# Output experts of the gated attention, batches 0 to 2: from all experts on all rows to rows sorted by chosen expert

## The chip, the cores and the metric

The program runs on one core of one Trainium2 chip. The metric is the device time of one execution in microseconds (us). Below, PE is TensorE, DVE is VectorE, ACT is ScalarE, POOL is GpSimd and SP is SyncE, which issues most of the DMAs.

## The reference, cut to what matters

```python
def _L0_ffn_ref(x, w_q, w_k, w_gate, value_experts, output_experts):
    ...
    gates = jax.nn.sigmoid((x @ w_gate).reshape(b, n, HEADS, EXPERTS).transpose(0, 2, 1, 3))
    sel = jnp.argmax(gates, axis=-1)
    gm = jax.nn.one_hot(sel, EXPERTS, dtype=x.dtype) * gates
    values = jnp.einsum('bhne,ehdk,bnd->bhnk', gm, value_experts, x)
    ...
    out = jnp.einsum('bhij,bhjk->bhik', attn, values)
    out = jnp.einsum('bhne,ehkd,bhnk->bhnd', gm, output_experts, out)
    return out.sum(axis=1)
```

This is the second of four layers: a cross-attention ("a"), this gated causal self-attention ("b"), a second cross-attention of 16 heads ("c"), and a layer of 32 routed experts ("d"). There are 4 batches of 512 tokens of 256 numbers. Layer b has 8 heads of 64 numbers, and for each token and head one of 8 experts is chosen: `gm` has one number per (token, head, expert) that is not zero. The last einsum turns a head's 64 numbers into 256 by the chosen expert's 64x256 matrix, scales them by its gate, and the sum over heads is added to x.

## The kernel before, in words

Layers a and b are in `attentions_ab`, which runs batch by batch: `attention_a(b)`, `head_b(b)`, `attention_b(b)`. Each engine has its own hand-written list of steps, and the lists meet at semaphores. Layers c and d follow in functions of their own.

In `attention_b` the four pairs of heads are worked one after the other. A pair's stretch of PE's list holds: 8 value units of the next pair (`unit`, L856: tokens of one tile times the 8 experts' value weights, 512 columns; DVE multiplies by the gates, L1209, and adds the 8 experts up, L1213); the transposes of the probabilities (`turn_b`, L794), read out by ACT (L1103) and DVE (L1319); the next pair's scores (`scores_b`, L773 and L778), whose maxima DVE takes (L1200) and whose exponentials ACT makes (L1095); probabilities times values (`values`, L827), read out by ACT into `boT` (L1125), which holds both heads of the pair, 64 partitions each; and the output experts. For these, DVE splits the gates over the softmax's sums into three bf16 parts (`split_gates`), PE transposes them (`gates`, L803) and spreads expert e's gates over the partitions (`select`, L814), DVE multiplies `boT` by them (`gate_out`, L1332), and PE multiplies each product by the expert's weights (`out`, L840):

```python
for t in range(NT):
    mm = pe.matmul(ps[:, 6 + t // 2, (t % 2) * D:(t % 2 + 1) * D], og[:, e, t * P:(t + 1) * P],
                   oxB[:, p, e, :], start=first and t % 2 == 0, ...)
```

All pairs and experts of a batch add up in PSUM banks 6 and 7, and DVE adds the sum to x at the start of the next batch (`add_out`, L1416). An fp32 matmul of the code stands as two MATMUL records in the trace; a transpose stands as one. The units of pairs 1 to 3 have a single PSUM bank (2), so a unit waits until DVE has multiplied the one before.

`unit` 0 to 7 and `pair` 0, 1, 2 come first; `last_pair` (pair 3) has no units and is filled with the scores of the next batch's layer a. In batch 3 `ending_pair` and the `quarter`s and `half`s of layer c take that place. SP loads the contexts (`load_context`, L516 to L520), x (L511) and the weights, and stores x (L581). POOL has the norms and little else in these batches.

## Time and profile before

| | |
|---|---|
| median of 3 runs | 2100.2 us (2096.24 to 2101.73) |
| profiled execution: span, from first to last instruction | 2122.9 us |
| the profiled execution's own time | no figure beside its span; the span stands for it |
| PE busy | 1982.3 us, 93% |
| DVE busy | 1269.1 us, 60% |
| ACT busy | 893.8 us, 42% |
| POOL busy | 528.3 us, 25% |
| DMA | 184.97 MB, 87 GB/s over the span |

Busy times of an engine are a union over the span. Layers a and b of the four batches lie between about 130 and 1100 us. A busy PE isn't PE at its peak: the granted clock tells the level.

### The profile page before, as it was taken

The page shows a single profiled execution, that of the slowest core. Times are in us where ns is not written, and L with a number is a line of the kernel's source. Part 1 is how long each engine was busy: PE and PEld are TensorE (multiplying, and loading weights), DVE is VectorE, ACT ScalarE, POOL GpSimd, SP SyncE. Part 2 cuts the span into 40 slices and gives each one's busy share as a digit, 9 for nine tenths or more (in the row PEclk, how much of TensorE's full clock was granted, in tenths as well). Part 3 has the DMA queues.
Part 4 walks back from the last instruction along what each step waited for, and adds up shares of the span by engine and source line. Part 5 has one row for each costly group of instructions (what it writes and reads, how often), then busy time and mean ns, then how long its engine had stood idle before and what let it go on. Part 6 is the DMA issues. An engine that isn't in the chain of part 4 may idle for free. (4 is left out here: it accounts for less than half of the span.)

```text
span 2122.9 us, 27241 instructions
## 1 busy us (share of the span) xinstructions
PE 1982.3 (93%) x10186; PEld 1100.5 (52%) x10186; DVE 1269.1 (60%) x2541; ACT 893.8 (42%) x1791; POOL 528.3 (25%) x454
## 2 busy tenths in 40 slices
PE   7989999999999999899989999999999999965994
PEld 5666567745676567746643333433433343334773
DVE  5423765366633764367777777777776777741343
ACT  3412211221112211121118888778777977841221
POOL 4311000210001000000034223236324531426664
PEclk9999999999999999999999999999999999986997
DMA  8743000110001000110226383345335432215986
GB/s 286 213 200 111 1 1 11 45 43 1 1 21 62 1 1 11 34 28 16 44 79 129 85 259 81 80 120 123 90 70 146 104 57 43 73 62 164 251 182 157
DMA packets 101531, 184.97 MB, mean 87 GB/s; under 512 B 38151, under 2 KB 62549, under 8 KB 100120
## 3 DMA queue, kind: packets, MB, share of 16 engines
q1 hardware_dynamic: 83000, 153.24, 26.8%
q0 software_dynamic: 18400, 30.00, 6.3%
q8 instruction: 81, 1.33, 0.3%
q14 instruction: 50, 0.41, 0.1%
HBM read 127.38 MB, written 65.25 MB: 91 GB/s over the span
## 5 line engine op out<-in xcount | busy, mean ns | idle before, releaser
L2216 DVE CUSTOM_DVE_ANT_0 ps<-ps,maskN 128x801 f32<-128x801 f32 x480 | 467.7, 1014 | 129.5 <-PE ps L2009 126.3
L2189 ACT ACTIVATE d_prob<-ps 128x512 f32<-128x512 f32 (+1 forms) x832 | 473.4, 597 | 158.3 <-PE ps L2039 153.2
L856 PE MATMUL ps<-vx_or_keys,b_xT 128*128 128x512 f32 x512 | 240.3, 597 | 4.9 <-DVE val_or_prob L1209 4.9
L840 PE MATMUL ps<-oxB,og_or_pT 128*128 128x256 f32 x1024 | 241.1, 380 | 0.0
L2051 PE MATMUL ps<-d_prob,vaug 128*32 128x512 f32 (+1 forms) x1664 | 226.6, 610 | 0.3 <-ACT d_prob L2189 0.3
L840 PEld LDWEIGHTS ps<-oxB,og_or_pT 128*128 128x128 f32 x1024 | 190.5, 190 | 37.4 <-issue 11.2
L2038 PE MATMUL ps<-maskT,identb 128*128 128x512 bf16 (+1 forms) x498 | 192.2, 386 | 5.7 <-DVE d_oN L2248 1.7
L1095 ACT ACTIVATE prob_or_gate<-ps,b_mx 128x512 f32<-128x512 f32 (+3 forms) x128 | 66.1, 525 | 289.4 <-DVE b_mx L1200 289.4
L2185 ACT CAST ps<-maskT 128x512 f32<-128x512 bf16 (+1 forms) x310 | 185.6, 599 | 0.0
L260 POOL DMA_INDIRECT table<-xr,slot x128 | 128.6, 1005 | 177.5 <-PE ps L2039 140.8
L1209 DVE TENSOR_TENSOR val_or_prob<-ps,b_gm 128x512 f32<-128x512 f32 x128 | 88.4, 691 | 107.1 <-PE ps L856 107.0
L856 PEld LDWEIGHTS ps<-vx_or_keys,b_xT 128*128 128x128 f32 x512 | 93.5, 190 | 85.5 <-issue 77.5
L1213 DVE TENSOR_REDUCE val_or_prob<-val_or_prob 128x64 f32<-128x512 f32 x128 | 132.3, 1034 | 4.4
L2039 PE MATMUL ps<-raw,kS 99*128 99x512 bf16 (+1 forms) x312 | 115.7, 387 | 1.7 <-ACT ps L2185 1.7
L2038 PEld LDWEIGHTS ps<-maskT,identb 128*128 128x128 bf16 (+1 forms) x498 | 49.7, 100 | 123.0 <-issue 36.6
L1913 POOL TENSOR_SCALAR maskT<-c_rawT 128x512 bf16<-128x512 int32 (+1 forms) x52 | 100.2, 1926 | 49.0 <-PE ps L2039 42.2
L2039 PE MATMUL ps<-vx_or_keys 99*128 99x512 bf16 (+1 forms) x260 | 99.2, 385 | 1.9 <-ACT ps L2185 1.9
L2039 PE MATMUL ps<-qS,vx_or_keys 99*128 99x512 bf16 (+1 forms) x260 | 98.9, 384 | 1.9 <-ACT ps L2185 1.9
L670 PE MATMUL ps<-og_or_pT,raw 128*128 128x128 f32 (+1 forms) x832 | 97.6, 275 | 0.0
L640 PE MATMUL ps<-maskN,kS 128*128 128x512 f32 (+1 forms) x256 | 95.0, 519 | 1.7 <-PEq L98 1.7
L670 PEld LDWEIGHTS ps<-og_or_pT,raw 128*128 128x128 f32 (+1 forms) x832 | 95.4, 192 | 1.5 <-issue 1.5
L1332 DVE TENSOR_TENSOR og_or_pT<-b_oT,ps 128x512 f32<-128x512 f32 x128 | 81.9, 681 | 18.2 <-PE ps L814 18.2
(321 smaller groups left out, 2807.8 us busy)
## 6 DMA issues: line engine op xcount, KB each, us to landing
c_rawT<-in_maskT SPq DMA_DIRECT2D x24, 512.0 KB
vx_or_keys<-k_parts SPq DMA_DIRECT2D x60, 200.1 KB, 7.2
k_parts<-x_k SPq DMA_DIRECT2D x16, 600.4 KB
table<-xr POOLq DMA_DIRECT2D x16, 578.0 KB
e_buf<-table SPq DMA_DIRECT2D x32, 289.0 KB
...
```

The costliest lines, as they stand in the source:

```text
L260: g.indirect_dma_start(out=k.table[:, :], out_offset=bass.IndirectOffsetOnAxis(ap=k.slot[:, j:j + 1], axis=0), in_=k.xr[:, t, :], in_offse ...
L670: mm = pe.matmul(ps[:, 6, m * P:(m + 1) * P], k.ctxNA[0:KW[i], i, m * P:(m + 1) * P], pT[0:KW[i], i, :], start=i == 0 and m == 0, stop=i = ...
L840: mm = pe.matmul(ps[:, 6 + t // 2, (t % 2) * D:(t % 2 + 1) * D], og[:, e, t * P:(t + 1) * P], oxB[:, p, e, :], start=first and t % 2 == 0, ...
L856: mm = pe.matmul(ps[:, bank, :], xTB[:, c, t * P:(t + 1) * P], vxB[:, c, h, :], start=c == 0, stop=c == NC - 1)
L1213: v.tensor_reduce(val[:, t, h // 2 % 2, h % 2, :], tmp[:, u % 2, :].rearrange("p (e d) -> p d e", e=EB), AX_X, ALU.add).then_inc(val_sum, 1)
L1913: g.tensor_scalar(maskT[0:KW[i], i, :], rawT[0:KW[i], u % 2, i % 2, :], 0.0, MASKED, ALU.is_equal, ALU.mult).then_inc(biasT, 1)
L2038: pe.matmul(ps[0:w, BANKS[u], :], k.identb[0:w, 0:w], maskT[0:w, i, :], start=True, stop=False)
L2039: pe.matmul(ps[0:w, BANKS[u], :], kS[G % NS][0:KROWS + 3, h, i * P:i * P + w], qS[G % NS][0:KROWS + 3, h, :], start=False, stop=True, skip ...
L2051: mm = pe.matmul(ps[VW * h:VW * (h + 1), ACC, :], vaug[0:w, G % 2, i, h, :], prob[0:w, T % 2, h, :], start=i == 0, stop=i == NKT - 1)
L2185: nc.scalar.copy(ps[0:w, BANKS[later], :], maskT[0:w, i, :]).then_inc(mask_a, 1)
L2189: nc.scalar.activation(prob[0:w, T % 2, h, :], ps[0:w, BANKS[GH * T + h], :], ACT.Exp, scale=SCALE_C).then_inc(exped, 1)
L2216: v.tensor_tensor_reduce(banks, banks, maskN[:, t, MO[half]:MO[half] + w], 1.0, -3.0e38, ALU.add, ALU.max, mp[:, t, h, half:half + 1]).the ...
```

## The change

`SORTED` is 3: for batches 0 to 2 the output experts work on sorted rows; batch 3 keeps the code above. For each head the 512 tokens are put in blocks of 128 rows with one expert's weights; 8 experts need at most `BLOCKS` = 11 of them (`ROWS` = 1408). Once in a batch PE counts (`counts`, 14 matmuls of 64 columns in bf16) and DVE works out each token's slot, its row numbers and each block's expert (`place`, 23 instructions in five pieces between the units 3 and 7, and one copy of the picks). Then for each pair Q = 4b+p: PE transposes `boT` back to tokens (`turn_rows`, 4), DVE scales by gate over sum (`weigh`) into `rows` (`write_rows`), POOL scatters them to DRAM with 8 indirect DMAs of 128 rows of 256 bytes, SP loads all 11 blocks (`load_sorted`, 704 KB) and, for 11 blocks and 2 heads, reads the expert's number into a register and loads 64x256 weights (`load_experts`). One pair later PE transposes the 11 blocks (`turn_sorted`, 3 groups), ACT reads them out (`read_sorted`), PE multiplies 22 times with 64 rows and 256 columns (`out_sorted`, 6 chunks), ACT reads each chunk out (128x1024) and stores it with two DMAs (`read_blocks`), POOL gathers 8 times 128 rows of 1 KB (`gather`), and DVE adds them to x with 8 additions of 128x256 (`add_back`), two pairs after Q.

`pair` becomes `sorted_pair`; `last_pair` has `turn_sorted` and `out_sorted` of pair 2 in the place of `out`, `select` and `gates`. Pair 3's sorted work stands in `sorted_between`, after the next batch's `attention_a` and ahead of its `head_b`. x has three buffers, in place of two; layer c's first queries move from batch 1 to batch 2; `oxB` is loaded once batches 0 to 2 are done with its memory; both `sorted_in` tensors are filled with zeros at the start.

```diff
+SORTED = NB - 1
+BLOCKS = (S + EB * (P - 1)) // P
+ROWS = BLOCKS * P
+CHUNKS = -(-BLOCKS // 2)
+PLACING = 23
...
+            def load_experts(b, p):
+                Q = PAIRS * b + p
+                sp.wait_ge(placed, PLACING * (b + 1))
+                if Q >= 2:
+                    sp.wait_ge(blocks_mm, CHUNKS * (Q - 1))
+                for j in range(BLOCKS):
+                    for a in range(2):
+                        at = (2 * p + a) * BLOCKS + j
+                        e = sp.value_load(of_block[b % 2][0:1, at:at + 1], min_val=0, max_val=EB - 1)
+                        half = slice(DB * a, DB * (a + 1))
+                        sp.dma_start(we[half, Q % 2, j, :], A["B_ox"][half, p, bass.ds(e, 1), :].rearrange(
+                            "p o n -> p (o n)")).then_inc(ld_we[Q % 2], 16)
+            def load_sorted(b, p):
+                Q = PAIRS * b + p
+                sp.wait_ge(scattered[Q % 2], 16 * 2 * NT * (Q // 2 + 1))
+                if Q:
+                    sp.wait_ge(sorted_mm, 3 * Q)
+                sp.dma_start(inS, k.sorted_in[Q % 2].rearrange("(j p a) d -> p j (a d)", p=P, a=2)).then_inc(ld_sorted, 16)
...
+                if b < SORTED:
+                    for p in range(PAIRS):
+                        load_experts(b, p)
+                        load_sorted(b, p)
+                        if p == 1 and b >= 1:
+                            keep_x(b - 1)
+                else:
+                    sp.wait_ge(blocks_mm, CHUNKS * EARLIER)
+                    for p in range(PAIRS - 1):
+                        sp.dma_start(oxB[:, p], A["B_ox"][:, p]).then_inc(ld_ox, 16)
                     first_group()
...
+            def scatter(b, p):
+                Q = PAIRS * b + p
+                g.wait_ge(placed, PLACING * (b + 1))
+                g.wait_ge(rows_v, Q + 1)
+                if Q >= 2:
+                    g.wait_ge(ld_sorted, 16 * (Q - 1))
+                for t in range(NT):
+                    for a in range(2):
+                        at = t * HB + 2 * p + a
+                        g.indirect_dma_start(out=k.sorted_in[Q % 2][:, :], out_offset=bass.IndirectOffsetOnAxis(
+                            ap=to_sorted[b % 2][:, at:at + 1], axis=0), in_=rows[:, t, a, :], in_offset=None,
...
+            def gather(Q):
+                b, p = divmod(Q, PAIRS)
+                all_kept(g, Q + 1)
+                for t in range(NT):
+                    n = NT * Q + t
+                    if n >= 2:
+                        g.wait_ge(added, 2 * (n - 1))
+                    for a in range(2):
+                        at = t * HB + 2 * p + a
+                        g.indirect_dma_start(out=back[:, t % 2, a, :], out_offset=None, in_=k.sorted_out[Q % 2][:, :],
+                                             in_offset=bass.IndirectOffsetOnAxis(ap=from_sorted[b % 2][:, at:at + 1], axis=0),
...
+                if b >= 1:
+                    g.wait_ge(nb.turned, b + 1)
+                for p in range(PAIRS):
+                    if b >= 1 and p < 2:
+                        gather(PAIRS * b - 2 + p)
+                    if b < SORTED:
+                        if p >= 2:
+                            gather(PAIRS * b - 2 + p)
+                        scatter(b, p)
...
+            def turn_sorted(Q, g):
+                if g == 0:
+                    pe.wait_ge(ld_sorted, 16 * (Q + 1))
...
+                if g == 2:
+                    pe.wait_ge(sorted_a, 3 * Q + 1)
+                for i, j in enumerate(range(4 * g, min(4 * g + 4, BLOCKS))):
+                    mm = pe.transpose(ps[:, 3 + g % 2, i * P:(i + 1) * P], inS[:, j, :], k.ident[:, :])
+                mm.then_inc(sorted_mm, 1)
+            def out_sorted(Q, c):
+                b, p = divmod(Q, PAIRS)
+                bank = 6 if p < PAIRS - 1 or c % 2 == 0 else 0
+                if c == 0:
+                    pe.wait_ge(sorted_a, 3 * (Q + 1))
+                    pe.wait_ge(ld_we[Q % 2], 16 * 2 * BLOCKS * (Q // 2 + 1))
...
+                before = CHUNKS * Q + c - (1 if p < PAIRS - 1 or c == 0 else 2)
+                if before >= 0:
+                    pe.wait_ge(blocks_a, before + 1)
+                for i, j in enumerate(range(2 * c, min(2 * c + 2, BLOCKS))):
+                    for a in range(2):
+                        half = slice(DB * a, DB * (a + 1))
+                        mm = pe.matmul(ps[:, bank + a, i * D:(i + 1) * D], inT[half, j, :], we[half, Q % 2, j, :],
+                                       start=True, stop=True)
+                mm.then_inc(blocks_mm, 1)
...
+            def sorted_between(b):
+                Q = PAIRS * b - 1
+                for g in range(3):
+                    turn_sorted(Q, g)
+                for c in range(CHUNKS):
+                    out_sorted(Q, c)
...
             for b in range(NB):
                 attention_a(b)
+                if b:
+                    sorted_between(b)
                 head_b(b)
...
+            def read_sorted(Q, g):
+                if g == 0 and Q % PAIRS < PAIRS - 1:
+                    act.wait_ge(placed, PLACING * (Q // PAIRS + 1))
+                act.wait_ge(sorted_mm, 3 * Q + g + 1)
+                w = min(4, BLOCKS - 4 * g)
+                nc.scalar.copy(inT[:, 4 * g:4 * g + w, :], ps[:, 3 + g % 2, 0:w * P].rearrange("p (j n) -> p j n", n=P)).then_inc(
+                    sorted_a, 1)
+            def read_blocks(Q, c):
+                p = Q % PAIRS
+                bank, n = 6 if p < PAIRS - 1 or c % 2 == 0 else 0, CHUNKS * Q + c
+                act.wait_ge(blocks_mm, n + 1)
+                if n >= 2:
+                    act.wait_ge(kept[c % 2], 32 * (n // 2))
+                if c < 2 and Q >= 2:
+                    act.wait_ge(gathered[0], 64 * (Q - 1))
+                    act.wait_ge(gathered[1], 64 * (Q - 1))
+                w = min(2, BLOCKS - 2 * c)
+                o = outS[p < PAIRS - 1][c % 2]
+                nc.scalar.copy(o[:, :, 0:w, :], ps[:, bank:bank + 2, 0:w * D].rearrange("p a (j n) -> p a j n", n=D)).then_inc(
+                    blocks_a, 1)
+                act.wait_ge(blocks_a, n + 1)
+                for a in range(2):
+                    half = k.sorted_out[Q % 2][ROWS * a:ROWS * (a + 1), :].rearrange("(j p) n -> p j n", p=P)
+                    nc.scalar.dma_start(half[:, 2 * c:2 * c + w, :], o[:, a, 0:w, :]).then_inc(kept[c % 2], 16)
...
                 for p in range(PAIRS):
                     Q, more = PAIRS * b + p, p + 1 < PAIRS
+                    behind = p >= 1 and b < SORTED
                     read_turned(Q)
+                    if behind:
+                        read_sorted(Q - 1, 0)
                     if more:
                         probabilities(b, p + 1, 0)
                     act.wait_ge(bpv_mm, Q + 1)
-                    if Q:
-                        act.wait_ge(gated, EB * Q)
+                    if 1 <= Q <= EARLIER:
+                        act.wait_ge(rows_mm, Q)
...
                     nc.scalar.copy(boT[:, :], ps[:, 5, :]).then_inc(bo_ev, 1)
+                    if behind:
+                        read_sorted(Q - 1, 1)
+                        read_sorted(Q - 1, 2)
+                        read_blocks(Q - 1, 0)
                     if more:
                         probabilities(b, p + 1, 1)
+                    if behind:
+                        for c in range(1, 4):
+                            read_blocks(Q - 1, c)
+                    if more:
                         probabilities(b, p + 1, 2)
+                    if behind:
+                        for c in range(4, CHUNKS):
+                            read_blocks(Q - 1, c)
             for b in range(NB):
                 attention_a(b)
+                if b:
+                    for g in range(3):
+                        read_sorted(PAIRS * b - 1, g)
+                    for c in range(CHUNKS):
+                        read_blocks(PAIRS * b - 1, c)
                 attention_b(b)
...
+            def write_rows(b, p):
+                Q = PAIRS * b + p
+                v.wait_ge(weighted, Q + 1)
+                v.wait_ge(rows_mm, Q + 1)
+                if Q:
+                    v.wait_ge(scattered[(Q - 1) % 2], 16 * 2 * NT * ((Q - 1) // 2 + 1))
+                v.tensor_tensor(rows, ps[:, 4, :].rearrange("p (t a d) -> p t a d", t=NT, a=2),
+                                weight.unsqueeze(3).to_broadcast([P, NT, 2, DB]), ALU.mult).then_inc(rows_v, 1)
+            def add_back(Q, t):
+                b, n = Q // PAIRS, NT * Q + t
+                x = k.xx[b % 3][:, t, :]
+                v.wait_ge(gathered[t % 2], 32 * (n // 2 + 1))
+                for a in range(2):
+                    if n or a:
+                        v.wait_ge(added, 2 * n + a)
+                    v.tensor_tensor(x, x, back[:, t % 2, a, :], ALU.add).then_inc(added, 1)
...
+            def sorted_pair(b, p):
+                u, Q = 2 * NT * (p + 1), PAIRS * b + p
+                def add(t):
+                    if Q >= 2:
+                        add_back(Q - 2, t)
+                unit(b, u)
+                turned_b(b, p, 1)
+                turned_b(b, p, 3)
+                unit(b, u + 1)
+                turned_b(b, p, 5)
+                weigh(b, p)
+                maxima(b, p + 1, 0)
+                unit(b, u + 2)
+                add(0)
+                unit(b, u + 3)
+                write_rows(b, p)
+                add(1)
+                unit(b, u + 4)
+                maxima(b, p + 1, 1)
+                unit(b, u + 5)
+                add(2)
+                unit(b, u + 6)
+                maxima(b, p + 1, 2)
+                unit(b, u + 7)
+                add(3)
...
```

The order of PE's instructions in batch 0, pair 1, from unit u+4 on. Before (L856 is `unit`, L773 and L778 the scores, L814 `select`, L840 `out`):

```order
L856 MATMUL ps<-vx_or_keys,b_xT 128x512 [waits b_val_mul]
L856 MATMUL ps<-vx_or_keys,b_xT 128x512
L773 MATMUL ps<-b_kT,b_qT 128x384 [waits b_exp]
L773 MATMUL ps<-b_kT,b_qT 128x384
L773 MATMUL ps<-b_kT,b_qT 128x128 x2
L778 MATMUL ps<-causal,identb 128x128 x4
L814 MATMUL ps<-b_gT,sel 128x512 [waits b_gated] x2
L840 MATMUL ps<-oxB,og_or_pT 128x256 [waits b_gated]
L840 MATMUL ps<-oxB,og_or_pT 128x256 x3
L856 MATMUL ps<-vx_or_keys,b_xT 128x512 [waits b_val_mul]
```

Now (L1056 is `unit`, L902 and L907 the scores, L992 `out_sorted`; `e_blocks` counts ACT's readouts):

```order
L1056 MATMUL ps<-vx_or_keys,b_xT 128x512 [waits b_val_mul]
L1056 MATMUL ps<-vx_or_keys,b_xT 128x512
L992 MATMUL ps<-oxB,og_or_pT 128x256 [waits b_val_mul,e_ld_we0,e_sorted]
L992 MATMUL ps<-oxB,og_or_pT 128x256 x3
L902 MATMUL ps<-b_kT,b_qT 128x384 [waits b_exp]
L902 MATMUL ps<-b_kT,b_qT 128x384
L902 MATMUL ps<-b_kT,b_qT 128x128 x2
L907 MATMUL ps<-causal,identb 128x128 x4
L992 MATMUL ps<-oxB,og_or_pT 128x256 [waits e_blocks]
L992 MATMUL ps<-oxB,og_or_pT 128x256 x3
L1056 MATMUL ps<-vx_or_keys,b_xT 128x512 [waits b_val_mul]
```

Where `out` waited for DVE's products, each chunk from the second on waits for ACT's readout of the one before.

ACT's order between the last step of `attention_a(1)` (L435) and layer b's first readout (L1388), where before the change nothing stood in between (`e_kept0` and `e_kept1` count landed stores; the rows L1379 and L1384 come 6 times in all):

```order
L435 COPY a_kb<-ps 128x4 [waits na_kb_mm]
L1365 COPY og_or_pT<-ps 128x512 [waits e_sorted_mm] x2
L1365 COPY og_or_pT<-ps 128x384 [waits e_sorted_mm]
L1379 COPY val_or_prob<-ps 128x1024 [waits rows_gathered0,rows_gathered1,e_kept0,e_blocks_mm]
L1384 DMA sorted_out<-val_or_prob 128x2x256 [waits e_blocks]
L1384 DMA sorted_out<-val_or_prob 128x2x256
...
L1379 COPY val_or_prob<-ps 128x2x256 [waits e_kept1,e_blocks_mm]
L1384 DMA sorted_out<-val_or_prob 128x256 [waits e_blocks]
L1384 DMA sorted_out<-val_or_prob 128x256
L1388 COPY b_xT<-ps 128x512 [waits nb_turned]
```

Six readouts and twelve stores of pair 3 now stand ahead of the copy that the gates, queries and keys of layer b wait for.

SP's order at the start of `load_experts(0, 0)`; the four rows from the register load on come 264 times in the program, 22 times for a pair:

```order
L558 DMA raw<-in_ctx 65x256
L603 TENSOR_LOAD oxB [waits e_placed]
L603 ISA x2
L605 ISA
L605 DMA oxB<-in_B_ox 64x256
L603 TENSOR_LOAD oxB
```

Before, SP had four loads of 1 MB for all batches (L563) in their place.

## Rows read from the trace of the kernel before

**Rows 1.** The page: the span and busy times of the engines.

```profile
span 2122.9 us, 27241 instructions
PE 1982.3 (93%) x10186; PEld 1100.5 (52%) x10186; DVE 1269.1 (60%) x2541; ACT 893.8 (42%) x1791; POOL 528.3 (25%) x454
```

**Rows 2.** Windows: stretch, its length, busy us of PE, PEld, DVE, ACT, POOL; clock; DMA.

```profile
206.90:225.60 18.70, 17.70 (x57) 7.30 (x56) 16.32 (x21) 4.40 (x16) 0.00 (x0) 1.00 0.00 1
225.60:260.30 34.70, 33.35 (x140) 18.40 (x141) 25.59 (x39) 6.42 (x20) 0.00 (x0) 1.00 0.00 0
260.30:298.10 37.80, 37.80 (x169) 23.65 (x168) 25.01 (x38) 6.53 (x20) 0.00 (x0) 1.00 0.00 1
335.90:367.10 31.20, 31.20 (x153) 23.44 (x152) 10.74 (x21) 3.82 (x6) 0.00 (x0) 1.00 0.01 1
```

**Rows 3.** PE's timeline in pair 1 of batch 0: start, length, line, tiles, count.

```profile
260.33 0.93 PE L794 MATMUL ps<-ident,prob_or_gate 128*128 128x128 f32 x7
261.09 1.89 PE L840 MATMUL ps<-oxB,og_or_pT 128*128 128x256 f32 x8
262.82 0.93 PE L794 MATMUL ps<-ident,prob_or_gate 128*128 128x128 f32 x7
...
282.14 0.59 PE L814 MATMUL ps<-b_gT,sel 128*128 128x512 bf16 x2
282.58 1.89 PE L840 MATMUL ps<-oxB,og_or_pT 128*128 128x256 f32 x8
...
289.99 0.70 PE L773 MATMUL ps<-b_kT,b_qT 64*128 64x256 f32 x4
290.62 0.29 PE L778 MATMUL ps<-causal,identb 128*128 128x128 bf16 x2
```

**Rows 4.** Groups on DVE and ACT by form, 200 to 1100 us.

```profile
L1213 DVE TENSOR_REDUCE val_or_prob<-val_or_prob 128x64 f32<-128x512 f32 x128 | 132.3, 1034 | 4.4
L1209 DVE TENSOR_TENSOR val_or_prob<-ps,b_gm 128x512 f32<-128x512 f32 x128 | 88.4, 691 | 107.1 <-PE ps L856 107.0
L1416 DVE TENSOR_TENSOR xx<-xx,ps 128x256 f32<-128x256 f32 x8 | 2.8, 415 | 4.8 <-PE ps L840 4.7
L1229 DVE TENSOR_TENSOR b_gr<-b_gr,gp 128x64 f32<-128x64 f32 x16 | 3.6, 225 | 0.5
L1245 DVE TENSOR_TENSOR prob_or_gate<-prob_or_gate,b_gtop 128x256 f32<-128x256 f32 x3 | 1.3, 425 | 0.1
L1070 ACT ACTIVATE val_or_prob<-ps,a_mx 128x1601 f32<-128x1601 f32 x12 | 19.2, 1597 | 109.0 <-DVE a_mx L1180 109.0
L1125 ACT COPY b_oT<-ps 128x512 f32<-128x512 f32 x16 | 9.4, 586 | 29.3 <-PE ps L827 29.3
```

**Rows 5.** Queries by line: DMA issues (duration ns min/median/max), a register move, landing times.

```profile
L294 SPq DMA_DIRECT2D total<-xr x3: 376/377/386, 1333.9 to 1738.3; - x3
DMA to landing us min/median/max: 2.9/2.9/4.0
L260 POOLq MOVE  x128: 29/29/29, 1410.5 to 1929.7; - x128
L260 POOL DMA_INDIRECT table<-xr,slot x128: 967/975/1607, 1411.3 to 1945.4; - x128
DMA to landing us min/median/max: 2.1/2.1/2.4
L516 SPq DMA_DIRECT2D maskN<-in_ctxT x6: 327/379/433, 160.4 to 641.3; - x6
DMA to landing us min/median/max: 4.2/5.0/7.1
```

**Rows 6.** PE's timeline and windows at the head of batch 3, where PE had waited.

```profile
899.62 0.69 PE L739 MATMUL ps<-ident,og_or_pT 128*128 128x128 f32 x2 [4.61 <-DVE og_or_pT L1159]
901.18 3.65 PE L745 MATMUL ps<-wgB,b_xT 128*128 128x64 f32 x16 [0.87 <-DVE b_xT L1287]
890.00:900.00 10.00, 4.93 (x37) 4.25 (x36) 5.16 (x8) 0.63 (x2) 3.71 (x4) 0.91 0.64 147
900.00:910.00 10.00, 9.13 (x26) 5.83 (x25) 5.17 (x9) 1.57 (x3) 0.00 (x0) 0.58 0.73 97
```

327 lines of the change are left out of this document (271 added, 56 removed).

## The prediction

> **What bounds the kernel now.** I read the page first, for the shares, then the windows by stage, then PE's timeline inside one pair, then the groups of DVE and ACT, and last the DMA issues. The page has PE busy 93% of a span of 2122.9 us [rows 1]. The windows show that in the stretches that the change touches it is full: in a middle pair PE is busy 37.8 of 37.8 us, in the last pair 31.2 of 31.2, while DVE has 25.0 and 10.7 and ACT 6.5 and 3.8 [rows 2]. Only the first units of a batch are another matter: DVE is busy 16.3 of 18.7 us and PE idles there [rows 2]. So in the pairs, work taken from PE is worth its time, as long as what replaces it keeps up; DVE has some 12 us of room in a pair, and ACT, POOL and SP are nearly idle. What has to be read out of the change is what these idle engines are asked to do in series with PE.
>
> **What PE loses and gets.** In PE's timeline eight records of `out` (one expert, four tiles) start 1.73 us before the next group, and two `select` start 0.44 before theirs [rows 3]. A pair gives up 8 x 1.73 + 8 x 0.22 + about 0.25 for the gate transposes = 15.8 us. It gets 4 + 11 transposes at 0.11 (seven take 0.76 [rows 3]) = 1.65, and 22 matmuls of 64 rows and 256 columns, 44 records. Four such records of the scores take 0.63 us, 0.158 each, against 0.216 for one of 128 rows [rows 3]: 7.0 us. So 8.7 us are added and 7.1 us a pair saved; over 12 pairs 85 us, less some 2 us for the counts. If PE stayed full, the kernel would lose 83 us. I expect that nearly all of it is given back, stage by stage.
>
> The trace has the two half-height tiles at 0.158 against 0.216, a factor of 1.37 and not 2 [rows 3]. The Trainium skill (TensorEngine Tiling (Array Packing), Theoretical Speedup) gives up to 2 for a contract dimension of at most 64; by that the 44 records would take 4.8 us and a pair would save 9.3. The sum goes by the row.
>
> **First units and placing.** `place` and its copy are 24 DVE instructions between the units, where DVE is the fuller engine: 5 of 64 columns at 0.225, 4 of 256 at 0.425 [rows 4], 13 short ones at about 0.2, and two of 704 columns at about 1.0 (0.691 for 512 [rows 4], scaled): 7.4 us. Some of DVE's 2.4 us of room takes part of it; I take +6 us a batch (bounds: +4, +7.4).
>
> **Pair 0.** Its stretch has four `out`, so PE's 34.7 us [rows 2] lose 6.9 + 1.8 + 0.25 and get 0.45: 26 us, or -8.7. DVE's 25.6 us [rows 2] lose eight products (0.69 each, the shape of L1209) and the splits and get 8 additions at 0.415 [rows 4] and one product: about 23, nearly as long as PE's. Bounds: -8.7 and, if the two only take turns, -5.
>
> **Pairs 1 and 2.** PE's own work becomes 37.8 - 15.8 + 8.7 = 30.7. Two losses come with it. The `out`s had filled PE while ACT and DVE read the transposes out; pair 0, without them, shows 1.35 us idle [rows 2], so +1.3. And a chunk can't start before ACT has read the one before out of the same banks: a readout of 1024 columns is 1.06 us (0.586 for 512 and 1.597 for 1601 [rows 4], a line through both), the two stores behind it 0.38 each, as the stores of L294 with rows of 1 KB [rows 5], together 1.9 us of ACT. A unit (1.72) between two chunks covers that, but chunk 1's readout stands behind the exponentials that wait for DVE's maxima, and chunk 4 has only scores ahead of it: I reckon 2.6 us. That gives 34.6, -3.2 each (bounds: -7 with no such wait, 0 with ACT late all along).
>
> **Last pair.** PE's own work falls to about 17 us (12 `out` go), but there are no units to put between the chunks: some 12 us of transposes, scores and values, then six rounds of 1.3 on PE, 1.06 on ACT and 0.2 of handing over, and the next batch's first exponential (1.6 us [rows 4]) stands behind the last store on ACT. I get 28.6 us, -2.6 (bounds: -8, +2).
>
> **Between the batches.** The largest loss. Here PE has nothing else: `head_b` stands behind `sorted_between`, and ACT's first readout for it behind six readouts and twelve stores. Each readout also waits for the landing of the stores two chunks back; a store of that kind lands 2.9 us after its issue [rows 5]. A chunk then costs (1.06 + 0.1 + 0.76 + 2.9) / 2 = 2.4 us, six of them with 2.3 of transposes ahead and ACT's copy behind some 17 us, where about 2 passed: +15 us for batches 1, 2 and 3 each (bounds: +9, PE's own work, and +19).
>
> **The sum.** A batch: +6 - 8.7 - 6.4 - 2.6 = -11.7, and +15 between: +3.3; three times, +10. PE's holes then cost clock. At the head of batch 3, after 4.6 us idle, the granted clock of the next 10 us was 0.58, mostly the lower of its two levels, 1.2 and not 2.4 GHz, and 16 short matmuls took 3.65 us [rows 6]. I put 3 us on each of the three places: +9. Batch 3 gets the additions of pairs 10 and 11 on DVE in its first two pairs: +2.
>
> **SP, the price that no row has.** For each pair SP does 22 times a register load, three register operations and a DMA. The DMA is 0.38 us [rows 5]; a register operation about 0.03, as POOL's moves [rows 5]. The register load has no row: it is at least such a move, 0.03, and at most a whole DMA round trip, 2.1 us [rows 5]. I take 0.8: it must go to memory and back like the DMA, but without descriptors and completion. So 1.27 us an item, 28 us a pair; the blocks' load behind it lands after about 5 us, as the 800 KB of L516 [rows 5]: 33.5 us after pair 0 starts, when `turn_sorted` in pair 1 wants them at 26 + 7 = 33. It just holds, +1 us a batch, +3. The Trainium skill (DMA: Bandwidth & Descriptors, Latency and other measured facts) gives a `tensor_load` floor of about 600 ns; by that an item would take 1.07 us and those 3 us would go.
>
> POOL has 16 indirect DMAs a pair at 0.98 us [rows 5], 16 us of 35. Its scatter stands behind a gather whose later tiles wait for DVE's additions; rows then are in DRAM some 26 us after a pair's start, ahead of SP's turn, so it costs nothing while SP is slower. If SP is quick, this is late next, by a few us in the last pair.
>
> Together +10 + 9 + 2 + 3 = +24 us: a span of 2147 us. The profiled span is 22.7 us (1.1%) above the median of the runs shown; on the median I forecast 2100.2 + 24 = **2124 us**. A change under 0.3% (6 us) can't be told from none.
>
> **Rivals.**
> - *SP becomes the bound* (0.25). If a register load takes 1.3 us, an item takes 1.8 and a pair 40 us. Then the first load of blocks is late by 12 us, the next by about 6, the last pair's by 9: +27 a batch, +81: 2205. It decides from about 1.3 us an item. For it: 264 items and one queue. Against: the wait of a batch's first items begins early, and pair 3's load has all of `attention_a` to hide in.
> - *PE keeps its gain: faster* (0.20), the other side. If the stores' landing and the exponentials hold ACT up less than I think, so that a pair runs at 32 us (-6 twice), the last at 25 (-6) and the part between costs +11, then a batch has 6 - 8.7 - 12 - 6 + 11 = -10, and with little lost to the clock the whole is -30 to -45: about 2062. For it: ACT has 31 of 38 us free in a pair now [rows 2]. Against: it isn't ACT's share but its place in the chain that counts, above all between the batches. It decides where ACT's turn for a chunk falls under PE's chunk and unit.
> - *It comes out even* (0.10): the half-height matmuls overlap by the full factor of 2. The chunks in nine pairs that PE waits on get 2.2 us shorter: -20, and 2104. The row of 0.158 speaks against it [rows 3]. The rule of the Trainium skill named above (TensorEngine Tiling (Array Packing), Theoretical Speedup) is what would make it so.
> - *The forecast* (0.45): slower by 10 to 50 us. All four assume that the sorted part does what it says; the 11 blocks are run whatever the picks are, so the picks can't shorten it.
>
> **How the numbers follow.** Faster by over 0.3%: the rival's 0.20 and 0.04 of the even case, 0.24. Within: 0.08, the even case and the forecast's lower edge. Slower: 0.68. The range reaches from 2060, the faster rival, to 2215, the SP rival with a dearer load; below lies a PE that stays full (2100 - 65), above a load near 2 us, together under 0.2. The likeliest case alone spans 2110 to 2150.
>
> **What would show it right or wrong.** PE idle some 8 us or more in each `sorted_between`, released by ACT, with the granted clock lower behind it; 64x256 matmuls at about 0.16 a record; middle pairs near 34.6 us and first units near 25; ACT's stores about 0.38. SP's items at 1.27 us; if PE's longest waits are for `inS` or `we`, the SP rival holds. I'm wrong if the middle pairs run at 31 us, or if the part between costs under 10.

## The result, and the profile after

| | median, us | runs | profiled span |
|---|---|---|---|
| before | 2099.6 | 4 (2096.2 to 2101.7) | 2122.9 |
| change | 2153.3 | 4 (2146.7 to 2158.9) | 2153.8 |

The ratio is 1.0256, 95% interval 1.0233 to 1.0279: slower by 53.7 us, where I had +24. The two profiled spans differ by 30.9 us only. That is no agreement with +24, since the profile of before stands 23 us over its median and the other stands at its own. The stages show it: the first weight load of layer c's score line (L2009 before, L2443 after) starts at 1102.2 us before and at 1150.5 after, +48.3 in the layers that the change touches, while the last layer, from its first transpose on, takes 208.4 us in the profile of before and 193.1 in that of after. The experiments come back to those 208 us.

The page of after, against [rows 1]:

```profile
span 2153.8 us, 29336 instructions
PE 1934.9 (90%) x10024; PEld 1024.5 (48%) x10024; DVE 1250.2 (58%) x2553; ACT 980.3 (46%) x1899; POOL 729.6 (34%) x660
```

PE has lost only 47 us of busy time, not the 83 of the reckoning, because part of its work now runs at the lower clock: over layers a and b, from the first unit of batch 0 on, the granted clock is 0.93, where it was 0.99. Windows of after, columns as in [rows 2] (first units and pair 0 of batch 0, pair 2 of batch 0, then of batch 1 pairs 0, 1 and 3, and the part between batches 0 and 1):

```profile
202.30:226.20 23.90, 20.11 (x75) 8.55 (x74) 21.29 (x42) 4.40 (x16) 0.00 (x0) 1.00 0.00 1
226.20:255.80 29.60, 25.59 (x97) 11.68 (x96) 20.46 (x29) 6.54 (x20) 8.01 (x8) 0.94 0.19 53
290.70:322.90 32.20, 29.11 (x148) 15.17 (x146) 20.41 (x31) 13.02 (x28) 16.05 (x16) 1.00 0.57 174
480.00:506.90 26.90, 24.95 (x98) 11.70 (x97) 22.10 (x34) 6.53 (x20) 10.02 (x10) 0.95 0.26 75
506.90:545.80 38.90, 32.67 (x152) 16.46 (x151) 22.37 (x34) 13.61 (x29) 18.11 (x19) 0.96 0.55 164
580.90:617.00 36.10, 24.61 (x113) 13.34 (x112) 10.04 (x21) 11.70 (x16) 17.75 (x18) 0.75 0.70 204
417.40:436.10 18.70, 12.68 (x80) 9.25 (x78) 0.69 (x1) 8.54 (x12) 1.22 (x2) 0.78 0.45 152
```

The pairs read against stages that were full: 37.8 of 37.8 in a middle pair [rows 2], now 32.67 of 38.9 or 29.11 of 32.2. The granted clock is still 1.00 in two of these rows, and lowest, 0.75 and 0.78, in the two where PE is busy least, 24.61 of 36.1 us and 12.68 of 18.7. The boundaries of all stages, from PE's timeline (us; three numbers are batches 0, 1, 2; the last column is the best kernel of the experiments, e14):

| stage | before | foreseen | after | e14 |
|---|---|---|---|---|
| first units | 20.5 each | 26.5 | 23.9, 25.6, 25.4 | 23.9, 29.5, 29.5 |
| pair 0 | 32.9 each | 24.2 | 29.6, 26.9, 26.9 | 29.6, 26.9, 26.9 |
| pair 1 | 37.8 each | 34.6 | 34.9, 39.0, 40.4 | 34.7, 34.3, 35.2 |
| pair 2 | 37.8 each | 34.6 | 32.2, 35.0, 32.4 | 32.2, 32.2, 32.2 |
| last pair | 31.2 each | 28.6 | 34.7, 36.1, 34.1 | 30.1, 28.6, 26.9 |
| layer a, then keys to gates, into 1 and 2 | 61.4 + 3.7, 57.0 + 3.7 | +15 each | 59.8 + 18.7, 64.1 + 20.4 | 58.7 + 3.7, 62.6 + 3.7 |
| the same into batch 3, in one | 56.8 | +15 | 69.7 | 55.9 |
| gates to first unit, into 1, 2, 3 | 15.6, 15.6, 19.2 | +3 each | 18.3, 18.7, 17.3 | 15.6, 15.6, 19.0 |

PE's timeline in the last pair of batch 1:

```profile
598.52 1.14 PE L992 MATMUL ps<-oxB,og_or_pT 64*128 64x256 f32 x8
600.77 1.14 PE L992 MATMUL ps<-oxB,og_or_pT 64*128 64x256 f32 x8 [1.11 <-ACT og_or_pT L1379]
...
606.01 2.08 PE L992 MATMUL ps<-oxB,og_or_pT 64*128 64x256 f32 x8 [1.86 <-ACT og_or_pT L1379]
609.20 2.08 PE L992 MATMUL ps<-oxB,og_or_pT 64*128 64x256 f32 x8 [1.11 <-issue]
612.39 1.22 PE L992 MATMUL ps<-oxB,og_or_pT 64*128 64x256 f32 x4 [1.11 <-ACT og_or_pT L1379]
617.00 1.97 PE L779 MATMUL ps<-ident,val_or_prob 128*128 128x128 f32 x8 [3.39 <-ACT val_or_prob L1325]
```

PE waits for ACT's readout before each chunk but the first, the same eight records go from 1.14 to 2.08 us as the clock falls to its lower level, and 3.39 us pass before the next batch's first exponential has come. Between the batches (0 to 1) it is the same chain with two pairs of banks:

```profile
426.91 1.14 PE L992 MATMUL ps<-oxB,og_or_pT 64*128 64x256 f32 x8 [0.98 <-ACT val_or_prob L1379]
428.94 1.13 PE L992 MATMUL ps<-oxB,og_or_pT 64*128 64x256 f32 x8 [0.89 <-ACT val_or_prob L1379]
430.96 0.88 PE L992 MATMUL ps<-oxB,og_or_pT 64*128 64x256 f32 x4 [0.89 <-ACT val_or_prob L1379]
431.78 1.97 PE L867 MATMUL ps<-ident,og_or_pT 128*128 128x128 f32 x8
436.11 1.11 PE L874 MATMUL ps<-wgB,b_xT 128*128 128x64 f32 x4 [2.37 <-ACT b_xT L1388]
```

A chunk comes every 2.03 us, that is a readout of 1.01, two stores of 0.45 and 0.1 between them, and then PE waits another 2.4 us for ACT's copy for the head. And in pair 1 of batch 1, PE waits for the loaded rows:

```profile
511.58 0.82 PE L929 MATMUL ps<-ident,prob_or_gate 128*128 128x128 f32 x6
515.72 0.66 PE L970 MATMUL ps<-ident,oxB 128*128 128x128 f32 x4 [3.33 <-DMA oxB<-sorted_in]
516.31 1.74 PE L902 MATMUL ps<-b_kT,b_qT 64*128 64x512 f32 x4
```

The cause stands in POOL's timeline: the scatter is queued behind the gather of the older pair's fourth tile, and that waits for an addition on DVE.

```profile
496.77 1.01 POOL L692 DMA_INDIRECT val_or_prob<-sorted_out,oxB  x1 [2.47 <-DVE xx L1637]
498.09 1.01 POOL L692 DMA_INDIRECT val_or_prob<-sorted_out,oxB  x1 [0.30 <-issue]
499.41 1.03 POOL L677 DMA_INDIRECT sorted_in<-oxB  x1 [0.30 <-issue]
```

### The profile page after: what moved, and what is told of

Read it like the earlier page. It is cut to its first block and busy times, and to the rows that moved or that the text cites. A ratio compares the mean times of both kernels' runs of the same rounds, so it can differ in the third digit from the quotient of the medians.

```text
span 2153.8 us, 29336 instructions
## 1 busy us (share of the span) xinstructions
PE 1934.9 (90%) x10024; PEld 1024.5 (48%) x10024; DVE 1250.2 (58%) x2553; ACT 980.3 (46%) x1899; POOL 729.6 (34%) x660
## 3 DMA queue, kind: packets, MB, share of 16 engines
q1 hardware_dynamic: 121208, 179.21, 30.9%
## 5 line engine op out<-in xcount | busy, mean ns | idle before, releaser
L1056 PE MATMUL ps<-vx_or_keys,b_xT 128*128 128x512 f32 x512 | 253.5, 623 | 19.1 <-DVE val_or_prob L1511 18.9
L692 POOL DMA_INDIRECT val_or_prob<-sorted_out,oxB x96 | 98.7, 1028 | 359.6 <-DVE xx L1637 160.7
L1056 PEld LDWEIGHTS ps<-vx_or_keys,b_xT 128*128 128x128 f32 x512 | 92.1, 195 | 114.1 <-issue 79.1
L677 POOL DMA_INDIRECT sorted_in<-oxB x96 | 95.7, 997 | 110.0 <-DVE oxB L1627 81.4
L992 PE MATMUL ps<-oxB,og_or_pT 64*128 64x256 f32 x528 | 86.8, 452 | 41.8 <-ACT og_or_pT L1379 27.8
L766 PE MATMUL ps<-maskN,kS 128*128 128x512 f32 (+1 forms) x256 | 101.3, 545 | 1.7 <-PEq L103 1.7
```

What stands on the lines that cost most here:

```text
L766: mm = pe.matmul(ps[:, i, 0:KC[i]], k.qkA[:, c, t * P:(t + 1) * P], k.ctxTA[:, c, i * BANK:i * BANK + KC[i]], start=c == 0, stop=c == NC - 1)
L1056: mm = pe.matmul(ps[:, bank, :], xTB[:, c, t * P:(t + 1) * P], vxB[:, c, h, :], start=c == 0, stop=c == NC - 1)
```

## The experiments

Theory A: where no units stand between the chunks, ACT's turn for a chunk sets the time, and each hole costs clock behind it. Theory B: the landing of stores, or PE's own work, sets it. Theory C: the sorted rows come late behind POOL's queue. My SP rival: SP's items set it. The runs came in five sets; within a set all kernels ran on one chip, beside runs of the kernel before.

| set | kernel | median | ratio to before, 95% |
|---|---|---|---|
| 1 (before 2119.9) | e1 before, once more | 2118.1 | one run |
| 1 | e2 one store | 2249.4 | 1.0587 (1.0553 to 1.0622) |
| 1 | e3 next units | 2253.0 | 1.0610 (1.0559 to 1.0661) |
| 1 | e4 no gather | 2228.5 | 1.0495 (1.0465 to 1.0524) |
| 2 (before 2100.6) | e5 change | 2149.7 | 1.0221 (1.0196 to 1.0247) |
| 2 | e6 fixed experts | 2142.0 | 1.0194 (1.0177 to 1.0211) |
| 2 | e7 next units, one store | 2128.1 | 1.0124 (1.0093 to 1.0155) |
| 3 (before 2124.6) | e8 rows first | 2270.3 | 1.0668 (1.0636 to 1.0701) |
| 3 | e9 e7, rows and mask first | 2232.7 | 1.0485 (1.0438 to 1.0533) |
| 3 | e10 e9, last pair | 2218.0 | 1.0445 (1.0409 to 1.0480) |
| 4 (before 2099.3) | e11 change | 2145.9 | 1.0218 (1.0198 to 1.0237) |
| 4 | e12 = e8 | 2153.0 | 1.0263 (1.0246 to 1.0280) |
| 4 | e13 = e9 | 2117.7 | 1.0095 (1.0076 to 1.0113) |
| 4 | e14 = e10 | 2089.5 | 0.9958 (0.9938 to 0.9978) |
| 5 (before 2128.0) | e15 change | 2272.9 | 1.0678 (1.0648 to 1.0708) |
| 5 | e16 = e2 | 2263.3 | 1.0652 (1.0624 to 1.0679) |
| 5 | e17 next units, mask first | 2236.7 | 1.0517 (1.0457 to 1.0576) |
| 5 | e18 exponential early | 2262.0 | 1.0637 (1.0614 to 1.0660) |

**The baseline.** e1 is the kernel before.

> The kernel before, once more, with a profile. If the 22.7 us by which its profiled span stood above the median belong to the kernel, this span is again near 2123 us. If they belong to that one execution (its last layer took 242 us where the changed kernel's took 229), this span is 2098 to 2103 us with a last layer of 229 +-3 us, and the changed kernel is to be set against that: +54 us, not +31.

The span is 2116.3 us beside runs of 2118 to 2125: neither expectation as written (it counted the last layer from an earlier instruction, hence its 242 and 229 us). Layers a and b end at 1104.1 us (1102.2 in the first profile), the last layer takes 205.1 (208.4). So the long last layer is no accident of one execution; it seems to come with whatever makes before 2119.9 us in this set and 2100 in sets 2 and 4. No profile of before was taken in a set of the second kind. That its layers a and b are the same there isn't shown, but they leave little room: PE is busy 37.8 of 37.8 us in the middle pairs, and the granted clock stays at 1.00 from 195 to 898 us.

**The changed kernel in three sets.**

> The changed kernel again, beside the next two on one chip; the control that the first set lacked, where all three variants came out at 2228 to 2253 us with ratios of 1.05 to 1.06, although two of them do less. Theory D (the distance between before and change is one and the same, and the variants are worse): ratio 1.026 +-0.003 again. Theory E (SP's and ACT's sequencers stall for 0.7 us now and then while POOL writes descriptors and loads are in flight, and how much differs from chip to chip; in the first set a pair's 22 loads took 31 to 38 us of SP where the first profile has 27 to 30): a ratio between 1.03 and 1.07, with SP's loads again over 30 us a pair in the profile.

> The changed kernel as reference of this set. If SP's register instructions last 0.03 to 0.15 us throughout: ratio 1.022 to 1.026, 2147 to 2155 us. If dozens of them last 0.7 us while POOL issues indirect DMAs (as in the first and third set): ratio 1.06 to 1.07, 2250 to 2270 us, since the variants with less work came out at 1.045 to 1.067 there.

> The changed kernel as reference of this set. With no slowed register instructions: 2145 to 2154 us, ratio 1.022 to 1.026. With dozens of register instructions of 0.7 us while POOL issues indirect DMAs: 2250 to 2275 us, ratio 1.06 to 1.07.

In sets 2 and 4 it is the first result again within the noise, at 1.022 just under theory D's lower edge of 1.023. In set 5 it costs 1.068, at the upper edge of what was foreseen. The queries on the lines of `load_experts` of e15, all 264 items (duration ns min/median/max), and under them the same of e11:

```profile
L603 SPq FUSED_REGOPS  x264: 2/152/726, 231.5 to 974.7; - x132
L605 SPq MOVE oxB<-in_B_ox x264: 2/29/906, 232.3 to 975.1; - x132
```

```profile
L603 SPq FUSED_REGOPS  x264: 152/152/187, 232.2 to 871.4; - x132
L605 SPq MOVE oxB<-in_B_ox x264: 29/29/38, 233.0 to 871.8; - x132
```

The medians are the same, the longest are not: a register move takes 29 ns, but some take up to 0.9 us. Leaving out the register loads themselves, in e15 83 of SP's register instructions last over 0.3 us; in e2, e3, e8, e9, e10, e16, e17 and e18 between 80 and 98; in e4, without gathers, 62; in all profiles of the first result and of sets 2 and 4 none. All of them, 839 in ten profiles, fall within 3 us of an indirect DMA of POOL. That isn't only because POOL is seldom quiet: in e4, 408 of SP's 1058 such instructions lie that near, and all 62 slow ones do. POOL itself isn't slowed (0.985 us a scatter in e15, 0.982 in e11), but other engines stand still in the same stretches. At the start of pair 1 of batch 1 of e15, SP's slow instructions follow one another from 545.3 to 558.2 us; ACT has nothing but waits from 547.3 to 559.7, and PE stands 5.32 us for its readout, where 0.35 is usual.

```profile
553.29 1.70 PE L929 MATMUL ps<-ident,prob_or_gate 128*128 128x128 f32 x7
560.32 1.76 PE L929 MATMUL ps<-ident,prob_or_gate 128*128 128x128 f32 x7 [5.32 <-ACT b_pT L1358]
561.87 3.62 PE L1056 MATMUL ps<-vx_or_keys,b_xT 128*128 128x512 f32 x4
```

Layers a and b end at 1252.8 us in e15 and at 1148.1 in e11, +104.7; the last layer, which has its own indirect DMAs in both kernels, takes 208.3 against 188.1. Which of the engines is slowed first, and what makes a set so, the runs don't show. It isn't the chip alone: sets 2 and 3 ran on the one with the same number (12), and set 2 has no slow instruction where every profile of set 3 has 80 or more. So the expectations' "on a chip like the first" has to be read as "in a set like the first". Whether fewer register instructions would lessen it is untested, since e6 below ran in set 2 only. For the result, taken with before at 2099.6, sets 2 and 4 are the ones to compare with.

**The part between the batches.** In e3 and e17 `sorted_between` is gone, and its steps stand in `attention_b` of the next batch. The banks, the buffers (`bpT` for `inT`) and with them the waits change too; the moved chunks share one pair of banks:

```
 unit(b, 1)
+late(turn_sorted, 0)
 unit(b, 2)
...
 unit(b, 4)
+late(out_sorted, 0)
 scores_b(b, 0, 2)
 unit(b, 5)
+late(out_sorted, 1)
 unit(b, 6)
+late(out_sorted, 2, 3)
 unit(b, 7)
+late(out_sorted, 4, 5)
```

> The last pair's blocks of a batch are transposed and multiplied among the first units of the next batch, where DVE is the fuller engine, and not alone between the batches. Theory A (the +45 us between the batches are PE standing alone behind ACT's chain; in the first units PE has 8 us free of 25): between the batches about 2 us as before, first units +2 to +5 a batch: -30 to -42 us in all, 2112 to 2124. Theory B (work moved is work moved: PE's 8.7 us come back in full in the first units, and batch 3 waits for its weights, whose load is later by some 15 us): 3 x (-15 + 9) + 10 = -8 us.

> The last pair's blocks among the next batch's first units alone (with batch 3's mask and keys loaded ahead of its weights, without which 13.5 us are lost there), against e15. The part between falls from 16.5 to 19 us to 3.7 (in batch 3 to 8), that is -13 to -15 a batch, and head and queries behind it regain 3 us of clock in two batches; the first units get 4 to 5 us longer: -27 to -33 us.

e3 has no reference in its set. e17 against e15 is -36.2 us, a little past theory A's -27 to -33, and far past theory B's -8. The combined kernel shows the place; in e2 and e16 the stores are one:

```
-for a in range(2):
-    half = k.sorted_out[Q % 2][ROWS * a:ROWS * (a + 1), :].rearrange("(j p) n -> p j n", p=P)
-    nc.scalar.dma_start(half[:, 2 * c:2 * c + w, :], o[:, a, 0:w, :]).then_inc(kept[c % 2], 16)
+both = k.sorted_out[Q % 2].rearrange("(j p a) n -> p j (a n)", p=P, a=2)
+nc.scalar.dma_start(both[:, 2 * c:2 * c + w, :], o[:, 0:w].rearrange(...)).then_inc(kept[c % 2], 16)
```

> One store per chunk and not two: the two halves of a row lie side by side in DRAM (a row's number is 2 x slot + half), so 1 KB pieces become 2 KB and ACT issues 6 stores a pair and not 12. Theory A (where no units stand between the chunks, a chunk takes ACT's readout and its two stores, 1.01 + 2 x 0.45 = 1.9 us, and the next exponential stands behind them): 6 x 0.45 = 2.7 us less in each last pair and each part between the batches, 5.4 a batch, -16 us in all, between -10 and -18. Theory B (the landing of the stores or TensorE's own work sets the chunk): -3 to 0 us. If only the part between gains, -8.

> One store per chunk alone, against e15. In the runs with both edits a last pair was shorter by 1.7 to 2.6 us. The part between has 2.03 us a chunk, ACT's readout and two stores; with one store its banks still alternate, so a chunk costs PE 1.13 and ACT 1.01 + 0.39, 1.4 us: -3.5 there. Sum -5.5 a batch: -14 to -18 us. If the stores' landing then sets the chunk: -6 to -9.

> Both edits of the first set together: the last pair's blocks among the next batch's first units, and one store per chunk. Against the changed kernel on the same chip. Theory A: -30 to -50 us. If the time is set by SP and by stalls of the sequencers, less than -20.

e16 against e15 is -9.5, between "-14 to -18" and "-6 to -9", and the two intervals overlap: there is probably a gain, smaller than ACT's issue time. The traces say why. The stretches from keys to gates are shorter by 2.6 and 1.5 us, and the one into batch 3 by 2.9, 7.0 in all and not 10.5, because ACT now waits for the store two chunks back, which lands 2.8 us after its issue (ACT's timeline of e16):

```profile
457.25 1.01 ACT L1379 COPY val_or_prob<-ps 128x1024 f32<-128x1024 f32 x1 [0.62 <-DMA sorted_out<-val_or_prob]
458.29 0.37 ACTq L1383 DMA_DIRECT2D sorted_out<-val_or_prob  x1
459.49 1.01 ACT L1379 COPY val_or_prob<-ps 128x1024 f32<-128x1024 f32 x1 [1.23 <-DMA sorted_out<-val_or_prob]
```

The readouts of this part start 1.58, 2.29, 1.63, 2.25 and 1.65 us apart, 1.88 in the mean against 2.05 in e15. With one store the landing sets every second chunk, and 0.2 us a chunk is won where 0.6 was expected. Theory B's landing stood right behind ACT's issue time. e7 against e5 is -21.6, under the -30 to -50 of theory A. Its stages say why: the parts between fell to 3.7 us and the last pairs by 1.7 to 2.6, but in pair 0 of batch 3 PE stood 13.45 us behind a copy of DVE, which itself stood 14.96 for the mask, queued on SP behind the output experts' weights (PE's and DVE's timelines of e7):

```profile
959.86 1.12 PE L932 MATMUL ps<-ident,prob_or_gate 128*128 128x128 f32 x4 [13.45 <-DVE b_pT L1723]
956.70 1.00 DVE L1652 TENSOR_SCALAR maskN<-raw 128x1601 bf16<-128x1601 int32 x1 [14.96 <-DMA raw<-in_mask]
```

I had named that load in e3's theory B, with the weights as what would be late; it was the mask behind them. e9, e13 and e17 load mask and keys first.

**SP.** e6 takes no register load, so its blocks get constant experts' weights instead of the chosen ones.

```
-e = sp.value_load(of_block[b % 2][0:1, at:at + 1], min_val=0, max_val=EB - 1)
-sp.dma_start(we[half, Q % 2, j, :], A["B_ox"][half, p, bass.ds(e, 1), :]...)
+sp.dma_start(we[half, Q % 2, j, :], A["B_ox"][half, p, j % EB, :])
```

> SP loads no register: each block gets the weights of expert (block number mod 8), a constant; so blocks are multiplied with other weights than the picks ask for, and the output's expert part is another. 22 DMAs a pair stay. Theory E and my SP rival (SP's 27 to 38 us a pair set when the next sorted rows can be loaded, behind them in the same queue): SP's stretch falls to 12 us a pair, pairs 1, 2 and the last pair get shorter by 1 to 4 us each on a chip like the first and by 5 to 12 on one like the second: -15 to -90 us, at least half of what lies above 2147. Theory A (ACT's chain alone): within 5 us.

-7.6 us, and the two intervals overlap. PE's waits for the loaded rows are as long as before: 3.64 and 3.58 us in pairs 1 of batches 1 and 2, 3.57 and 3.51 in e5, and those pairs take 39.3 and 40.2 us (39.2 and 39.6). Where SP isn't slowed, its items aren't what PE waits for there. Theory A's "within 5" is missed narrowly, the SP rival's -15 by much.

**The gathers.** e4 issues none, so the experts' outputs are missing from its result.

> No rows are gathered (the additions read whatever stands in their buffer; the experts' outputs are missing from the result), the rest is as in the changed kernel. Theory C (pairs 1 and 3 of batches 1 and 2 are long because POOL's 8 gathers stand ahead of the scatter and the rows come back late): pairs 1 of batches 1 and 2 fall from 39 and 40 us to the 35 of batch 0, last pairs by 2 us: -10 to -20 us. Theory A (ACT's chain and the clock make them long): -3 to +1 us.

It ran in set 1, without a reference. Pairs 1 of batches 1 and 2 took 42.1 and 42.3 us there, pair 1 of batch 0 51.6: no answer to theory C, because the missing gathers take away slow stretches too. With half of the added indirect DMAs gone, 62 slow register instructions are left, where the other runs of these sets have 80 to 98.

**The late rows.** e8 and e12 put the scatter ahead of the fourth tile's gather.

```
-gather(PAIRS * b - 2 + p)
-scatter(b, p)
+gather(PAIRS * b - 2 + p, range(3))
+scatter(b, p)
+gather(PAIRS * b - 2 + p, (3,))
...
 turned_b(b, p, 5)
+if p and Q >= 3:
+    add_back(Q - 3, 3)
 weigh(b, p)
```

> The changed kernel, but POOL scatters a pair's rows ahead of the gather of the older pair's fourth tile, and DVE adds that tile early in the next pair (with that, the first batch's kept x is stored a pair later). Theory C (in batches 1 and 2 the scatter starts 3 to 4 us late, behind that gather, which waits for an addition, and PE then waits 3.3 to 3.6 us for the loaded rows in pair 1, with a clock penalty of 1 to 3 us behind it): pairs 1 of batches 1 and 2 fall from 39.2 and 39.6 us to 34.9 to 36: -6 to -9 us in all. If DVE's in-order additions only move the wait: 0 +-2 us, with waits of DVE for the fourth tile in the next pair.

> Rows scattered ahead of the fourth tile's gather, against e11 on the same chip. Theory C (late rows make pairs 1 of batches 1 and 2 long): -6 to -9 us, with those pairs at 35 to 36 us. If the wait only moves to DVE or SP: 0 +-2.

e12 against e11 is +7.1 us (their intervals don't overlap), and yet theory C is right at its place. In batch 1, pair 1 falls from 39.4 to 34.3 us and pair 2 from 34.9 to 32.2; PE's wait for the rows in pair 1 is gone (in batch 2, 1.86 us of 3.32 are left). It all comes back in the last pairs, 33.3, 33.1 and 34.1 us in e11, 38.7, 37.6 and 40.7 in e12. DVE's and PE's timelines of e12 there:

```profile
607.73 0.89 DVE L1639 TENSOR_TENSOR kS<-kS,val_or_prob 128x256 f32<-128x256 f32 x2 [12.55 <-DMA val_or_prob<-sorted_out,oxB]
608.54 1.82 DVE L1481 TENSOR_REDUCE a_mx<-ps 128x1 f32<-128x1601 f32 x1
612.57 1.76 PE L781 MATMUL ps<-ident,val_or_prob 128*128 128x128 f32 x7 [6.88 <-ACT val_or_prob L1327]
```

The fourth tile's addition now waits 12.55 us for a gather behind the scatter, and the maximum of the next batch stands behind that addition. The second half of my expectation, the wait that moves to DVE, had the mechanism; I had put it in the next pair.

**The last pair.** e18 has one edit, on DVE and ACT; e10 and e14 have it too, and DVE reads bank 7 of each chunk while ACT reads bank 6.

```
 write_rows(b, p)
 add_back(Q - 2, 1)
+maximum(b + 1, 0)
 add_back(Q - 2, 2)
 add_back(Q - 2, 3)
...
+if not more and b + 1 < NB:
+    exponential(b + 1, 0)
 if behind:
     for c in range(4, CHUNKS):
         read_blocks(Q - 1, c)
```

> Only this is changed: the next batch's first maximum stands ahead of the last two additions on DVE, its first exponential ahead of the last two chunks on ACT. PE's wait for that exponential (3.4 us in each of the three places) goes; ACT's 1.6 us stand in the chunks' chain instead: -1.5 to -3 us a batch, -5 to -9 us. If ACT's chain were off the path there: -10.

> All edits so far together: last pair's blocks among the next batch's first units, one store per chunk, rows scattered ahead of the fourth tile's gather; and in batch 3 the mask and keys are loaded ahead of the output experts' weights (in the run with the first two edits PE stood 13.5 us in batch 3's first pair, because DVE waited for that mask, issued behind the late weights). Against 2128 for the first two: -13 for the mask, -7 for the rows: 2105 to 2112 us, ratio 1.002 to 1.006. If the weights now come late instead: 2115 to 2122.

> The same, and in the last pair of batches 0 to 2: DVE reads half of each chunk (one bank of the two), and the first maximum and exponential of the next batch stand ahead of the last two chunks. Theory A as the runs have mended it (with one store, a chunk still takes PE 1.13, ACT 1.01 and two hand-overs, 2.25 us, because one pair of banks serves all chunks, then 3 to 4 us of exponential): a chunk falls to 1.8 us (-2.2 a batch) and PE no longer waits for the exponential (-3 a batch): -12 to -17 us against the run before, 2092 to 2098, that is faster than the kernel before. Rival (the loaded rows or the clock set the last pair): within -4 us.

> The last pair's blocks among the next batch's first units, one store per chunk, rows first, mask first, against e11 on the same chip. On a chip like the second set's: 2105 to 2112 us, -40 to -45 us against e11. On a chip like the first and third set's: 1.045 to 1.05 of before again, about -35 us.

> The same with DVE reading half of each chunk in the last pair and the next exponential ahead of the last two chunks. Theory A: -12 to -17 us against e13, 2092 to 2098 on a chip like the second set's: faster than before. In the third set it was -15.

e18 against e15 is -10.8, just past the -5 to -9, with intervals that overlap by a little; in all three places the transposes now follow the last chunk without a wait. e10 against e9 is -14.8, e13 against e11 -28.2 instead of -40 to -45 (it carries the price of rows first: its last pairs take 35.5, 38.3 and 40.3 us), and e14 against e13 -28.2, twice what I gave it. Its last pairs fall by 5.4, 9.7 and 13.4 us, which is more than the -12 to -17 in all of the expectation; that the early maximum, now ahead of the addition that waits, also removes that price is read from the order and not from a run of its own. PE's timeline of e14 in the last pair of batch 1, and the part between batches 0 and 1:

```profile
568.63 1.14 PE L1002 MATMUL ps<-oxB,og_or_pT 64*128 64x256 f32 x8
570.65 1.14 PE L1002 MATMUL ps<-oxB,og_or_pT 64*128 64x256 f32 x8 [0.88 <-DVE og_or_pT L1857]
...
577.44 2.08 PE L1002 MATMUL ps<-oxB,og_or_pT 64*128 64x256 f32 x8 [0.88 <-DVE og_or_pT L1857]
580.39 1.23 PE L1002 MATMUL ps<-oxB,og_or_pT 64*128 64x256 f32 x4 [0.87 <-DVE og_or_pT L1857]
581.55 1.75 PE L787 MATMUL ps<-ident,val_or_prob 128*128 128x128 f32 x7
...
410.82 1.84 PE L416 MATMUL ps<-bkA,b_kT 128*128 128x1 f32 x16
412.53 1.07 PE L877 MATMUL ps<-ident,og_or_pT 128*128 128x128 f32 x8
```

A chunk takes 2.02 us, not the 1.8 of the expectation, and no longer 2.25; PE goes from the last chunk to the next batch's transposes without a wait. The first units pay for the moved blocks: 29.5 us in batches 1 and 2, and 29.1 in batch 3, where 20.5 were before. Still layers a and b end at 1081.0 us, 21 earlier than before, in a profile whose run, 2081.8 us, was one of the fastest of e14's ten (2081.2 to 2097.8). e14 is the one version that beats both kernels: 0.9958 of before, 2089.5 us, and 56.4 under e11. This holds only in a set without the slow instructions: in set 3 the same kernel costs 1.0445.

## Why the prediction was wrong

**The sign was right, the size was half.** The forecast's mechanism, PE's gain given back stage by stage, held; two terms of its sum, the last pair and pair 1, failed. Against the +48.3 us of layers a and b:

- *Between the batches* (+45): measured +44.7 (+15.0, +16.8, +12.9). The total was right, partly by luck: a chunk takes 2.03 us and not 2.4, because the landing overlaps with ACT's issues, and the rest is the lower clock and ACT's late copy. The landing itself was priced well (2.9 us; 2.8 in e16), and e16 shows that it is next in line. e7 and e14 confirm the place: without `sorted_between` it is 3.7 us again.
- *Last pair* (-7.8): measured +11.3. **This is the step that failed most, by 19 us.** "Some 12 us of transposes, scores and values" ahead of the first chunk was too small: it starts 14.8, 17.6 and 15.7 us into the stage, behind waits for the readouts of the transposes (1.4 to 1.8 us) and, in batch 1, with a group of scores that took 3.62 us at the lower clock, not 1.88. The six rounds took 15.8, 15.1 and 15.1 us, as the 15.4 of the forecast (6 x 2.56). The exponential I had named and given no more than its own length, 1.6 us; the wait is 4.15, 3.39 and 3.35 us, because the last chunk's readout and stores stand ahead of it too. "PE's own work falls to about 17 us" left the clock out: in batch 1 PE is busy 24.6 us. e18 takes the wait for the exponential away by the order alone; with that order, one store and DVE's share of the readouts together (e14) the last pair of batch 1 takes 28.6 us.
- *Pair 1* (-9.6): measured +0.9. Batch 0 took 34.9, close to 34.6; batches 1 and 2 took 39.0 and 40.4, because PE waits 3.33 and 3.70 us for the rows, and the clock falls behind that. The prediction saw "a few us in the last pair" of it and looked in the wrong pair: POOL's gathers of the older pairs exist from pair 0 on in batches 1 and 2. e12 removes the wait in batch 1 and halves it in batch 2.
- *Pair 0* (-26): measured -15.4. The row that I took for it, 34.7 us, holds the last unit of the stage before; the pair is 32.9 us long. The bound "-5 if the two only take turns" was nearer: 26.9 us with DVE busy 22.1 and PE waiting for it.
- *Pair 2* (-9.6): measured -13.7; where no hole stands ahead of it, it takes 32.2 us. PE is busy 29.1 us of it where I had 30.7, and idle 3.1 where I had 3.9, so my 2.6 us for the chunk waits were somewhat too many. Eight records of the half-height matmuls go by in 1.06 us, 0.133 each and not 0.158. The rival with the full overlap would have 0.11; the Trainium skill (TensorEngine Tiling (Array Packing), Theoretical Speedup) gives up to 2 and the trace 1.6.
- *First units* (+18): +13.5. *Batch 3* (+2): +2.3. *Clock* (+9): gates to first units +3.9 and layer a of batches 1 and 2 +5.5, with one step of layer c's queries now in another batch. The start came 4.6 us earlier, which no term had. Neither the 3.9 nor the start is surely the change's: in e1, the kernel before, gates to first unit take 15.6 us in batch 0 and 18.9 in batches 1 and 2, where the first profile has 18.9 and 15.6.
- *SP* (+3): an item is 1.26 to 1.42 us, as 22 take 27.7 to 31.3, where I had 1.27. That it is so near is luck: the register load took 0.268 us and not 0.8, the DMA 0.469 and not 0.38, and one of the register operations 0.152 and not 0.03. The rival's bound of 1.3 an item is passed in eight of the twelve pairs and yet SP doesn't bound the kernel: e6 gains 7.6 us and leaves the waits for the rows as they were. In set 5, 22 items take 32.3 to 39.6 us.

The stages give +48.3 and the medians +53.7. I had set the sum against a median and a profile that belong to two kinds of sets, and without a profile of before in a set of the faster kind the 5.4 us between the two figures stay open.

**The rivals.** PE keeps its gain: false as predicted, but e14 reaches -10 us with the gain that this rival spoke of, once the chunks stand beside units and the exponential ahead of the readouts. In batch 1 of e14 the stages sum to -8.7 us, near its -10, but by other terms: +9.0 in the first units, nothing between the batches, and less won in the pairs. SP: false here. Even: false, though the matmuls it rested on are half as far from the full overlap as the row of before had them.
